# Row statistics of a fused attention and expert kernel: two tiles in one statistics instruction

## The reference

```python
def _layernorm(x, axis=-1, eps=1e-05):
    m = jnp.mean(x, axis=axis, keepdims=True)
    v = jnp.var(x, axis=axis, keepdims=True)
    return (x - m) / jnp.sqrt(v + eps)
...
h = _layernorm(x, axis=-1) * (1 + ca) + sa
x = x + ga * _L0_attn_ref(h, ...)     # linear attention, MLP, two inner layer norms with g1, b1, g2, b2
h = _layernorm(x, axis=-1) * (1 + cb) + sb
x = x + gb * _L0_ffn_ref(h, ...)      # softmax router, top-k per expert, gelu expert of 256 units
```

## Time and profile before

| | us |
|---|---|
| median of 3 runs | 235.41 |
| lowest and highest run | 235.26 and 235.48 |
| span of the profiled execution | 234.0 |
| between the profiled span and the median | 1.41 |
| DVE busy | 175.7 (75%) |
| PE busy | 178.5 (76%) |
| POOL busy | 152.0 (65%) |
| ACT busy | 132.5 (57%) |

### The profile page before, as it was taken

The page is one execution under the profiler, slowest core; times in us unless marked ns, Lnnn a source line. Parts: engine busy times, 40 slices in busy tenths (PEclk is TensorE's granted clock), DMA queues, the critical chain, the costliest instruction groups (busy, mean ns, idle before and its releaser), DMA issues.

```text
span 234.0 us, 4342 instructions
## 1 busy us (share of the span) xinstructions
PE 178.5 (76%) x1161; PEld 140.9 (60%) x1161; DVE 175.7 (75%) x661; ACT 132.5 (57%) x425; POOL 152.0 (65%) x236
## 2 busy tenths in 40 slices
PE   0789898999799999966467879877589989985000
PEld 0536676878579987864316365545379779974000
DVE  1889988699999999999998879999018997554000
ACT  2149985367546889873987763242537668851000
POOL 8698837357564666664599960047777777777771
PEclk9999999999979999995575557999999999999655
DMA  5995000000010000000067223003333342111110
GB/s 163 272 281 185 3 0 1 0 3 0 1 48 0 0 4 0 1 3 0 0 201 205 86 86 101 0 22 95 99 102 92 112 121 76 56 49 56 56 45 22
DMA packets 16967, 15.49 MB, mean 66 GB/s; under 512 B 1904, under 2 KB 14320, under 8 KB 16944
## 3 DMA queue, kind: packets, MB, share of 16 engines
q1 hardware_dynamic: 14288, 9.70, 14.1%
q0 software_dynamic: 2240, 5.51, 8.0%
q10 hardware_dynamic: 416, 0.01, 0.1%
HBM read 8.92 MB, written 6.29 MB: 65 GB/s over the span
## 4 chain that ended last, share of the span: by engine, by line
DVE 39%; PE 37%; issue 7%; ACT 7%; POOL 6%; DMA 2%; POOLq 1%; DVEq 0%; ACTq 0%
PE pH L974 7%; DVE x_sb L1190 6%; DVE scr L1312 6%; PE pQ L983 6%; POOL out_dram L422 5%; PE pQ L881 3%; DVE bn L1022 3%; DVE t L1134 3%; PE pQ L688 2%; DVE x_sb L1136 2%; DMA x_sb<-in_L_attn_x_dram 2%; DVE t L1132 2%; PE pH L804 2%; PE pH L871 2%; PE pQ L815 2%
## 5 line engine op out<-in xcount | busy, mean ns | idle before, releaser
L419 POOL DMA_INDIRECT rows<-table_dram,gidx x28 | 30.0, 1073 | 24.4 <-DVE gidx L1404 16.2
L422 POOL DMA_INDIRECT out_dram<-rows,gidx x28 | 27.4, 978 | 8.5 <-issue 6.4
L974 PE MATMUL pH<-x_sb,hid 128*128 (+1 forms) x140 | 22.5, 283 | 1.1 <-ACT hid L637 0.9
L983 PE MATMUL pQ<-ew,u 128*128 (+1 forms) x140 | 22.2, 281 | 1.2 <-ACT u L651 0.8
L983 PEld LDWEIGHTS pQ<-ew,u 128*128 128x128 f32 x140 | 18.4, 191 | 3.0 <-issue 1.9
L1453 DVE SCALAR_TENSOR_TENSOR t<-pQ,wslot,scr 128x128 f32<-128x128 f32 x35 | 12.3, 351 | 10.3 <-PE pQ L983 10.1
L651 ACT ACTIVATE u<-pH 128x256 f32<-128x256 f32 x35 | 13.4, 384 | 11.4 <-PE pH L974 11.3
L974 PEld LDWEIGHTS pH<-x_sb,hid 128*128 128x128 f32 x140 | 18.4, 191 | 2.2 <-issue 2.0
L524 ACT ACTIVATE sqj<-pQ 128x128 bf16<-128x128 f32 x60 | 15.8, 281 | 6.5 <-PE pQ L815 3.0
L287 POOL TENSOR_TENSOR yr<-yv,neghalf 128x4 f32<-128x4 f32 x16 | 17.0, 1065 | 1.3
L1022 DVE BATCH_NORM_STATS2 bn<-x_sb 128x6 f32<-128x128 f32 x64 | 13.8, 279 | 5.2 <-DMA x_sb<-in_L_attn_x_dram 5.0
(11 more groups left out here) (331 smaller groups left out, 537.7 us busy)
## 6 DMA issues: line engine op xcount, KB each, us to landing
table_dram<-x_sb SPq DMA_DIRECT2D x9, 256.0 KB, 2.8
x_sb<-in_L_attn_x_dram SPq DMA_DIRECT2D x8, 256.0 KB, 5.2
table_dram<-rows SPq DMA_DIRECT2D x7, 256.0 KB, 2.3
ew<-in_L_ffn_W_dram SPq DMA_DIRECT2D x2, 512.0 KB, 9.3
w1d<-in_L_ffn_W_dram SPq DMA_DIRECT2D x1, 1024.0 KB, 11.7
rows<-table_dram,gidx POOLq DMA_INDIRECT x28, 2.8
out_dram<-rows,gidx POOLq DMA_INDIRECT x28, 2.2
wmod_sb<-in_L_wmod_dram SPq DMA_DIRECT2D x1, 384.0 KB, 4.8
```

The lines of the kernel that those rows point to most:

```text
L419: gp.indirect_dma_start(row[:, t, :], None, table[:, :], bass.IndirectOffsetOnAxis(gidx[:, t:t + 1], 0)).then_inc(gathered[t], 16)
L422: gp.indirect_dma_start(out.rearrange("b l d -> (b l) d"), bass.IndirectOffsetOnAxis(gidx[:, t:t + 1], 0), row[:, t, D:2 * D], None).then_ ...
L974: mm = te.matmul(pH[i % 2][:, f * P:(f + 1) * P], wcur[:, i % RW, f * P:(f + 1) * P], xt[:, bass.ds(i - e, 1), :], start=True, stop=True)
L983: mm = te.matmul(pQ[i % 2][:, 0:D], eh[:, i % 2, f * P:(f + 1) * P], ew[:, bass.ds(e, 1), f * D:(f + 1) * D], start=(f == 0), stop=(f == 1))
```

## The change

One `bn_stats` now reads two neighbouring tiles, their elements in turn: tile 0 element 0, tile 1 element 0, tile 0 element 1, and so on. What it writes for the even elements is then the first tile's count, mean and sum of squared deviations, and what it writes for the odd ones is the second tile's. A group needs two such instructions of 256 elements, and no aggregation and no wait between. The means are read from `bn` where `mv` was read before. The variance is the sum of squared deviations over 128, so the scaling before the power multiplies by 1 / D instead of 1. The values of a group lie in `bn` as two by two, three apart, so the scaling and `nm` run over two by two elements.

```diff
-        bn = sb("bn", [P, G, GT, 6]); mv = sb("mv", [P, G, GT, 2]); ve = ...
+        bn = sb("bn", [P, G, GT // 2, 6]); ve = ...
...
+        def mean_of(g, t):
+            return bn[:, g, t // 2, 3 * (t % 2) + 1:3 * (t % 2) + 2]
+
+        def pairs(v):
+            return v.rearrange("p (a k) -> p a k", k=2)
+
+        def means(g):
+            return bn[:, g, :, 1:6:3]
+
+        def squares(g):
+            return bn[:, g, :, 2:6:3]
...
             def rsqrt(dst, src, tmp, scale, eps, width):
-                link(gp.tensor_scalar(tmp, src, scale, eps, ALU.mult, ALU.add))
+                link(gp.tensor_scalar(pairs(tmp), src, scale, eps, ALU.mult, ALU.add))
                 return gp.tensor_tensor(dst, tmp, neghalf[:, 0:width], ALU.pow)
...
-                rsqrt(rs[:, g, :], mv[:, g, :, 1], ve[:, g, :], 1.0, LN_EPS, GT).then_inc(S["rs1"], 1)
+                rsqrt(rs[:, g, :], squares(g), ve[:, g, :], 1.0 / D, LN_EPS, GT).then_inc(S["rs1"], 1)
...
             def stats(g, ready):
-                for t in range(GT):
-                    last = dve.bn_stats(bn[:, g, t, :], x_sb[:, g * GT + t, :])
-                link(last)
-                for t in range(GT):
-                    last = dve.bn_aggr(mv[:, g, t, :], bn[:, g, t, :])
-                return last.then_inc(S[ready], 1)
+                for a in range(GT // 2):
+                    two = x_sb[:, g * GT + 2 * a:g * GT + 2 * a + 2, :].rearrange("p t d -> p d t")
+                    last = dve.bn_stats(bn[:, g, a, :], two)
+                last.then_inc(S[ready], 1)
...
-                dve.scalar_tensor_tensor(nm[:, g, :], mv[:, g, :, 0], -1.0, rs[:, g, :], ALU.mult, ALU.mult).then_inc(S["nm_done"], 1)
+                dve.scalar_tensor_tensor(pairs(nm[:, g, :]), means(g), -1.0, pairs(rs[:, g, :]), ALU.mult, ALU.mult).then_inc(S["nm_done"], 1)
```

More of the change, by code:

```diff
@@ L104, in build @@
         scr = sb("scr", [P, 28, D])
-        bn = sb("bn", [P, G, GT, 6]); mv = sb("mv", [P, G, GT, 2]); ve = sb("ve", [P, G, GT]); rs = sb("rs", [P, G, GT]); nm = sb("nm", [P, G, GT])
+        bn = sb("bn", [P, G, GT // 2, 6]); ve = sb("ve", [P, G, GT]); rs = sb("rs", [P, G, GT]); nm = sb("nm", [P, G, GT])
         xn = rows2[:, 0, :, :].rearrange("p (g t) d -> p g t d", t=GT); h2T = sb("h2T", [P, 2, W]); hT = scr[:, 20:28, :].rearrange("p (a t) d -> p a (t d)", t=GT); ex = sb("ex", [P, 2, W])
@@ L290, in rs_a @@
                 gp.wait_ge(S["stats1"], g + 1)
[L291 removed]
+                rsqrt(rs[:, g, :], squares(g), ve[:, g, :], 1.0 / D, LN_EPS, GT).then_inc(S["rs1"], 1)
                 if g >= SHARED:
                     gp.wait_ge(S["rs1"], g + 1)
[L294 removed]
+                    gp.tensor_scalar(xn[:, g, GT - 1, :], x_sb[:, g * GT + GT - 1, :], mean_of(g, GT - 1), rs[:, g, GT - 1:GT],
                                      ALU.subtract, ALU.mult).then_inc(S["xn1_pool"], 1)
@@ L381, in yrs @@
                 of = slice(k * GT, (k + 1) * GT)
-                rsqrt(yr[:, g % RY, of], ssq[:, g % RY, of], yv[:, g % RY, of], 1.0 / D, LN_EPS, GT).then_inc(S[done], 1)
+                rsqrt(yr[:, g % RY, of], pairs(ssq[:, g % RY, of]), yv[:, g % RY, of], 1.0 / D, LN_EPS, GT).then_inc(S[done], 1)
             def rs3(g):
                 gp.wait_ge(S["stats3"], g + 1)
-                rsqrt(rs[:, g, :], mv[:, g, :, 1], ve[:, g, :], 1.0, LN_EPS, GT).then_inc(S["rs3"], 1)
+                rsqrt(rs[:, g, :], squares(g), ve[:, g, :], 1.0 / D, LN_EPS, GT).then_inc(S["rs3"], 1)
             def h2tok(g):
@@ L394, in h2tok @@
                     for t in range(GT):
-                        last = gp.tensor_scalar(xn[:, g, t, :], x_sb[:, g * GT + t, :], mv[:, g, t, 0:1], rs[:, g, t:t + 1],
+                        last = gp.tensor_scalar(xn[:, g, t, :], x_sb[:, g * GT + t, :], mean_of(g, t), rs[:, g, t:t + 1],
                                                 ALU.subtract, ALU.mult)
@@ L1020, in stats @@
             def stats(g, ready):
-                for t in range(GT):
-                    last = dve.bn_stats(bn[:, g, t, :], x_sb[:, g * GT + t, :])
-                link(last)
-                for t in range(GT):
-                    last = dve.bn_aggr(mv[:, g, t, :], bn[:, g, t, :])
-                return last.then_inc(S[ready], 1)
+                for a in range(GT // 2):
+                    two = x_sb[:, g * GT + 2 * a:g * GT + 2 * a + 2, :].rearrange("p t d -> p d t")
+                    last = dve.bn_stats(bn[:, g, a, :], two)
+                last.then_inc(S[ready], 1)
             def normalise(g):
                 for t in range(GT - 1 if g >= SHARED else GT):
-                    last = dve.tensor_scalar(xn[:, g, t, :], x_sb[:, g * GT + t, :], mv[:, g, t, 0:1],
+                    last = dve.tensor_scalar(xn[:, g, t, :], x_sb[:, g * GT + t, :], mean_of(g, t),
                                              rs[:, g, t:t + 1], ALU.subtract, ALU.mult)
```

## The result

| | us |
|---|---|
| median of the changed kernel, 4 runs | 231.88 (231.35 to 233.0) |
| median of the kernel before, beside it | 235.33 |
| ratio | 0.9859, 95% interval 0.9827 to 0.9891 |
| span of the profiled execution, before | 234.0 |
| span of the profiled execution, after | 231.3 |

A forecast was written before the change was run, and what follows sets the result against it. No engine bounds the whole: PE sets the pace from 63.6 to 80.8 us, DVE to 107.1. Savings of 0.20 + 0.20 + 0.35 + 0.20 = 0.95 us off 234.0, plus 1.41 carried over, gave 234.5 us; range 233.3 to 235.7.

The forecast's parts named there:

- list of places: Five stretches of the kernel where saved statistics time was judged to reach the path or not; sum 0.95 us.
- Hop at the reductions' price: New statistics instruction on DVE: length 585 ns, a group holds DVE 1.01 us, 0.20 us less than now.
- the lower end of the bounds: New statistics instruction with no cost for hopping: length 0.409 us, each group some 0.55 us less; whole kernel 233.5 us.
- the rival with a chance of 0.20: The hop costs nothing, since each interleaved stream walks forward one word at a time: 233.5 us, chance 0.20.
- s: The saving of one group's statistics on DVE, forecast at 0.20 us.
- Place 1: Group 0 of the first set: its statistics feed TensorE's first transposes, so all PE work after moves by s, 0.20 us.
- Place 2: Groups 4 to 6, first set, DVE 17.6 to 26.1 us: GpSimd is late next, so one s of three arrives.
- Place 3: 41 to 80.8 us: no statistics on the path; second set's groups 0 to 2 beside a never idle TensorE: 0.
- the clock as a rival: TensorE's half clock at 65 to 68 us cost 1.7 us; escaped 232.8, hit again 236.2 us; chance 0.10, half each way.
- Places 4 and 5: 80.8 us on, second set: groups 3 and 4 give 0.35 us (L796's limit), 5 nothing, 6 gives s, 7 nothing.
- After 107 us it is handed on one to one: Search, routing and experts each start from what comes last, so the 0.95 us saved passes through to the end.
- Edits costed at nothing: Other edits, such as two by two reads in GpSimd's scaling: taken as 0, bounded by 0 to 0.08 us per instruction.

The follow-up runs named there:

- prices: Changed kernel plus 13 groups of three extra DVE instructions at its end, in various element orders; three span 1.06 us in storage order, 1.07 for two alternating streams.
- slow_read: Changed kernel with the same statistics, but elements read in transposed order, each step 16 words on; 233.73 us beside 235.12, ratio 0.9933.
- first_only: Kernel before with the change made only in the first set (statistics of the input); 234.89 us beside 235.57, ratio 0.9974.
- again: Changed kernel run a second time without edit, with more runs; 232.94 us beside 235.12, ratio 0.9901.
- second_only: Kernel before with the change made only in the second set (statistics of x1); 233.56 us, ratio 0.9915.
- warm_fill: Changed kernel plus ten small unread PE matmuls before the first data and two more where PE waits for the first x1; 230.86 us, ratio 0.9796.
- before_again: Kernel before, unchanged, run again for a second profile; ratio 1.0004.
- before_fill: Kernel before plus two unread matmuls of 512 and 256 columns on PE where it waits for the first x1; ratio 0.9966.
- fill: Changed kernel plus two unread matmuls of 512 and 256 columns on PE where it waits for the first x1; 232.28 us beside 235.6, ratio 0.9857.
- warm: Changed kernel plus ten small unread matmuls on PE while it waits for the first data; 231.87 us beside 235.6, ratio 0.9839.
- late_more: Kernel before plus five unread matmuls of 512 columns on PE before the first expert item; ratio 0.9984.
- late_experts: Kernel before plus three unread matmuls of 512, 512 and 256 columns on PE before the first expert item; ratio 1.0017.

## Why the prediction was wrong, point by point

Three steps failed: the price of the new instruction, the zero for 41 to 80.8 us, and the handing on after 107 us. In the pair of profiles only the first and the third are at work. The list of places with the measured price gives 1.9 us, and the attention stages gave 1.9; the gathers added 1.2, by luck as far as the prediction goes, since it has no term for them. The second shows in profiles without the slow stretch.

**The price of the new instruction: wrong, and the first cause.** The step "Hop at the reductions' price" chose 585 ns; it is 420, the lower end of the bounds, the rival with a chance of 0.20. The reductions that served as the nearest rows step by 16 words in one stream; the new instruction alternates between two streams that each go on by one word, and this costs nothing (prices: 1.07 us for three beside 1.06). s is 0.53 us, not 0.20. slow_read shows that the reasoning on the price was right for a read that does hop.

**Place 1, group 0: right in the profile after,** 0.52 us for s, and 0.20 at the forecast price in slow_read. It holds only where the input lands late. In six other profiles with the fast first set it landed at 4.63 to 4.85 us instead of 5.08, and the stage took 3.47 to 3.82 us, not 3.44: POOL's own setup runs until some 5.75 us, and its scaling for group 0 starts no earlier in any of the six (at 5.85 in first_only, where DVE's result was complete at 5.43). The prediction has no such limit.

**Place 2, groups 4 to 6: right.** Of three savings one arrives: 0.75 us with s at 0.53, and 0.19 with s at 0.20. The 0.2 us above s is not resolved; first_only has it too (0.71).

**Place 3, "no statistics on the path", groups 0, 1 and 2 of the second set "beside a TensorE that is never idle", priced at 0: wrong where the slow stretch is absent, and the second cause.** In the profile of before TensorE ran at half the clock for 3.4 us of this stage. The prediction had the clock as a rival, but with one price, 1.7 us, for the stretch itself, as if the old kernel paid it in full. The runs show that it does not: when the slow stretch is absent, DVE with the old statistics is busy nearly all the time and the stage takes 49.4 us instead of 49.8. The new statistics give DVE 0.53 us per group there too, 47.6 us in the mean. So between x1 and the search the change is worth 0.6 us in profiles with the slow stretch and 1.8 in those without. Which of the executions without a profile had it is not known, so its share in the 3.45 us of the medians stays open.

**Places 4 and 5: right in the waits, nearly right in the sum.** L796 (L808 after) moved to its limit, L1176 (L1186) waits for ScalarE, POOL takes group 7 right after 6. The stage gave 0.66 us in the profile after; the list gives 0.35 + 0.53 less 0.1 = 0.78 at the measured price.

**"After 107 us it is handed on one to one": wrong, and the third cause.** Up to the first gather this holds within 0.2 us. Then POOL's 56 transfers, one behind the other, set the end, and the gathers have two lengths, some 38.5 and 37.4 us, that go with where a gather meets DVE's first copy of the item work, 0.17 or some 0.6 us ahead of it. In the profiles after, again, prices, second_only and warm_fill the expert items began 18.3 to 18.4 us after the first gather, with PE at half clock in its last dense matmuls (0.50 at 168 to 170 us in the profile after, 3.53 us for what took 2.02 before). In before, before_again, before_fill, first_only, slow_read, fill and warm there was no such stretch and they began after 16.7 to 16.8 us. So there 1.1 us of the gain came, as the profiles read, by way of a slower PE, which moved the items by 1.5 to 1.7 us and with them the meeting. The sixth profile with short gathers, late_more, had this slow stretch too (3.52 us for the same matmuls), so no profile has short gathers without it; late_experts and the meeting times speak for the moment and not for the clock as such, but no run separates the two. Why a gather is longer there stays open, and so does why the changed second set meets the slow stretch at 168 us more often; of the seven profiles with the new instruction and its fast read in the second set, these five had it, and before, before_again, before_fill and first_only did not.

**Edits costed at nothing: right where nothing disturbs them.** POOL's scaling of two by two elements takes 0.18 to 0.22 us then, as before, and `nm` 0.10 to 0.16. In the mean the scaling into `yv` went from 278 to 309 ns; that is within the 0 to 0.08 us that the prediction allowed.

**The range** ended at 233.3 us. It held the first cause alone, at 233.5, and left out the clock's 232.8; it never had the two together, and it had nothing for the gathers. By the measured price the list gives 1.0 us more than the forecast, a full clock 1.2 us more (1.8 instead of 0.6), and short gathers 1.1 us.

## What to carry to other kernels

Price a new access pattern by the number of streams that it walks and by the step within each, not by whether it hops. Before a stage is written off because an engine is never idle in it, ask whether that engine ran at its full clock in the one profile at hand, and price the stage without the slow stretch. Where an engine issues transfers one behind the other with a constant gap, it is the bound even if the chain of waits leads elsewhere; count its distances, and see what another engine does where they change.

## What the runs showed of the hardware

- Statistics and reductions on VectorE over 256 float32: two alternating streams, at 128 or 640 words, and every second word run like storage order (three in 1.06 to 1.08 us); four streams, or every fourth or 16th word, cost 1.54 to 1.61 us for three (prices).
- TensorE's granted clock fell to 0.50 (1.2 GHz) for 3.4 us, 1.1 to 2.1 us after it had started again behind 1.5 us of idleness, in five of the eleven profiles that have this idleness (before, before_again, after, again, first_only), and not in warm, prices, second_only, slow_read, late_experts and late_more. It did not fall in the three in which unread matmuls filled the idleness (fill, warm_fill, before_fill); three are too few to show that filling it prevents the fall.
- 28 indirect gathers on GpSimd took either 38.3 to 38.6 us (eight profiles) or 37.4 (six). In the eight a gather starts 0.17 or 0.18 us ahead of VectorE's first copy of 512 elements and takes 1.7 us instead of 0.95; in the six the nearest starts 0.58 to 0.63 us ahead. In both, gathers beside VectorE's item work end up at its distance of 1.34 us instead of their own 1.25.
